# A four-layer graph network on one core: the sum of the attention exponentials moved from GpSimd to VectorE

## The reference, cut to what matters

```python
h = x @ W_sa
s_left = h @ a_sa[0, :Hd]
s_right = h @ a_sa[0, Hd:]
scores = s_left[:, None] + s_right[None, :]
e = jnp.where(adj_a != 0, jnp.exp(-jax.nn.leaky_relu(scores, 0.01)), 0.0)
attn = e / (jnp.sum(e, axis=1, keepdims=True) + 1e-05)
x_a = attn @ h
x_b = adj_b @ (x @ W_gcnb) + b_gcnb
return jax.nn.sigmoid(attn_a * x_a + attn_b * x_b)
```

## Time and profile before

| what | us |
|---|---|
| median of 3 runs | 504.92 |
| the three runs | 504.92, 501.99, 504.94 |
| the profiled execution's own time | 503.84 |
| span of its records | 502.0 |

### The profile page before, as it was taken

One profiled execution on the slowest core, in us unless ns is written; L12 is line 12 of the kernel. 1 busy time (PEld: TensorE's weight loads), 2 busy tenths in 40 slices (PEclk: granted clock), 3 DMA queues, 4 the chain that ended last, 5 costly groups with the idle time before them and its releaser, 6 DMA issues.

```text
span 502.0 us, 5846 instructions
## 1 busy us (share of the span) xinstructions
PE 481.2 (96%) x1973; PEld 319.1 (64%) x1973; DVE 349.6 (70%) x757; ACT 243.8 (49%) x448; POOL 173.1 (34%) x175
## 2 busy tenths in 40 slices
PE   5999999999999989999999999999999999999994
PEld 4889855545555678878545445555556645878782
DVE  4589879999963569849233952972752289699984
ACT  5766549992877353433334533442433466343200
POOL 1421242460534028934000631451240055355531
PEclk9999999999999999999999999999999999999998
DMA  8757120000453000000000000000000000000000
GB/s 300 235 170 215 40 83 0 0 0 1 125 208 119 25 1 1 0 1 1 0 1 0 0 1 1 2 0 0 0 1 0 0 1 2 1 12 21 22 31 29
DMA packets 8149, 20.70 MB, mean 41 GB/s; under 512 B 976, under 2 KB 4708, under 8 KB 8120
## 3 DMA queue, kind: packets, MB, share of 16 engines
q1 hardware_dynamic: 6840, 18.75, 11.3%
q0 software_dynamic: 464, 0.79, 0.7%
q10 hardware_dynamic: 816, 0.79, 0.5%
HBM read 18.94 MB, written 1.39 MB: 40 GB/s over the span
## 4 chain that ended last, share of the span: by engine, by line
PE 77%; DVE 11%; issue 4%; ACT 3%; POOL 3%; DMA 1%; POOLq 0%; DVEq 0%; ACTq 0%
PE psum L1445 17%; PE psum L1227 10%; PE psum L1489 9%; PE psum L1263 9%; PE psum L1323 5%; PE psum L1555 4%; PE psum L1210 4%; PE psum L1425 4%; DVE ST L991 2%; PE psum L1282 2%; PE psum L1398 2%; PE psum L1144 2%; PE psum L1526 2%; DVE ST L987 1%; PE psum L1309 1%
## 5 line engine op out<-in xcount | busy, mean ns | idle before, releaser
L1445 PE MATMUL psum<-QT,xT 128*128 128x512 f32 (+3 forms) x264 | 108.7, 543 | 0.3 <-DVE xT L1026 0.3
L412 POOL TENSOR_TENSOR es<-es,ST 128x512 f32<-128x512 f32 (+3 forms) x60 | 72.9, 1215 | 53.7 <-ACT ST L617 52.4
L604 ACT ACTIVATE ST<-psum 128x512 f32<-128x512 f32 (+3 forms) x66 | 36.1, 547 | 84.1 <-DVE rm L965 80.3
L1445 PEld LDWEIGHTS psum<-QT,xT 128*128 128x128 f32 (+1 forms) x264 | 47.7, 186 | 40.9 <-issue 34.0
L965 DVE TENSOR_TENSOR rm<-psum,rm 128x512 f32<-128x512 f32 (+3 forms) x60 | 37.4, 624 | 41.7 <-PE psum L1445 41.4
L362 POOL TENSOR_TENSOR rstd<-veps,nhalf 128x1 f32<-128x1 f32 (+1 forms) x44 | 28.9, 658 | 94.9 <-DVE veps L772 94.8
L1555 PE MATMUL psum<-Wh,ST 128*128 128x256 f32 (+3 forms) x242 | 55.7, 381 | 1.0 <-DVE vbuf L1039 1.0
L1489 PE MATMUL psum<-ST,Wh 128*128 128x512 f32 (+3 forms) x132 | 54.4, 543 | 1.6 <-DVE vbuf L1012 1.1
L1263 PE MATMUL psum<-eb,x_all 128*128 128x512 f32 (+3 forms) x132 | 52.8, 545 | 0.0
L617 ACT ACTIVATE ST<-ST 128x512 f32<-128x512 f32 (+3 forms) x66 | 37.9, 579 | 27.4 <-DVE ST L987 24.8
L1555 PEld LDWEIGHTS psum<-Wh,ST 128*128 128x128 f32 (+3 forms) x242 | 44.3, 186 | 9.9 <-DVE vbuf L1039 1.8
(11 more groups left out here) (161 smaller groups left out, 788.2 us busy)
## 6 DMA issues: line engine op xcount, KB each, us to landing
adj_rows<-in_adj_dram SPq DMA_DIRECT2D x10, 677.0 KB, 5.6
rows<-in_adj_dram SPq DMA_DIRECT2D x10, 677.0 KB, 3.9
out_dram<-xs SPq DMA_DIRECT2D x10, 128.0 KB, 1.7
x_all<-in_x_dram SPq DMA_DIRECT2D x2, 512.0 KB, 6.8
W<-in_L_gnn_W_stack_dram SPq DMA_DIRECT2D x2, 512.0 KB, 6.2
adj_rows<-in_adj_dram SPq DMA_DIRECT2D x1, 338.5 KB
rows<-in_adj_dram SPq DMA_DIRECT2D x1, 338.5 KB
w0n<-in_L_gnn_weight_dram ACTq DMA_DIRECT2D x1, 256.0 KB, 5.2
```

The source lines that it names most:

```text
L412: nc.gpsimd.tensor_tensor(es[0:r, g % 2, 0:w], es[0:r, g % 2, 0:w], buf(g)[0:r, j, 0:w], ALU.add)\
L1445: last = nc.tensor.matmul(psum[0:r, SB[n % 3], 0:w], xT[l][:, k, j * P:j * P + r], QT[:, k, c0:c1], start=(k == 0), stop=(k == KD - 1))
```

## The change

The eleven additions to `esumb` leave GpSimd's program and enter VectorE's as `add_exps(j)`, with the same operands. Among the first six tiles `add_exps(j - 1)` stands behind `scores(j)`. `add_exps(5)` stands behind the 22 dot products and ahead of `scores(6)`. For the later tiles `add_exps(j - 1)` stands ahead of `scores(j)`, which is behind the two `zp_evac` of the round before. `add_exps(10)` stands behind the last `zp_evac` and ahead of the three `mean_mask`. The number of buffers stays at six, and the wait of `scores(j)` for `den_added` is now one for VectorE's own earlier work. TensorE's and ScalarE's programs are the same as before.

```diff
--- before.py
+++ after.py
@@ -368,16 +368,6 @@
                 r = kk(i)
                 pool.wait_ge(NA.x_ready.sem, T)
                 nc.gpsimd.tensor_scalar(xp5[0:r, i, :], x_all[0:r, i, :], 0.5, 1.0, ALU.add, ALU.mult).then_inc(xp5_ready.sem, 1)
-            for j in range(T):
-                r = kk(j)
-                pool.wait_ge(exp_ready.sem, j + 1)
-                if j == 0:
-                    nc.gpsimd.tensor_copy(esumb[:, 0:N], ebs[0][:, 0:N]).then_inc(den_added.sem, 1)
-                else:
-                    pool.wait_ge(den_added.sem, j)
-                    nc.gpsimd.tensor_tensor(esumb[0:r, 0:N], esumb[0:r, 0:N], ebs[j % RING][0:r, 0:N], ALU.add)\
-                        .then_inc(den_added.sem, 1)
-
             def low_half(i):
                 r = kk(i)
                 pool.wait_ge(xh_ready.sem, i + 1)
@@ -836,7 +826,6 @@
                 e = ebs[j % RING][0:r, 0:N]
                 if j >= RING:
                     dve.wait_ge(h_step.sem, j - RING + 1)
-                    dve.wait_ge(den_added.sem, j - RING + 1)
                 own.link(nc.vector.tensor_scalar(e, adjT[0:r, j, 0:N], 0.0, MASKED, ALU.is_equal, ALU.mult))
                 if j == 0:
                     dve.wait_ge(nslb_ready.sem, NC)
@@ -844,6 +833,17 @@
                                                         op0=ALU.add, op1=ALU.add))
                 nc.vector.scalar_tensor_tensor(out=e, in0=e, scalar=SLOPE, in1=e, op0=ALU.mult, op1=ALU.min)\
                     .then_inc(score_ready.sem, 1)
+
+            def add_exps(j):
+
+                r = kk(j)
+                dve.wait_ge(exp_ready.sem, j + 1)
+                if j == 0:
+                    nc.vector.tensor_copy(esumb[:, 0:N], ebs[0][:, 0:N]).then_inc(den_added.sem, 1)
+                else:
+                    dve.wait_ge(den_added.sem, j)
+                    nc.vector.tensor_tensor(esumb[0:r, 0:N], esumb[0:r, 0:N], ebs[j % RING][0:r, 0:N], ALU.add)\
+                        .then_inc(den_added.sem, 1)
 
             def zp_evac(i):
                 r = kk(i)
@@ -864,6 +864,8 @@
 
             for j in range(RING):
                 scores(j)
+                if j >= 1:
+                    add_exps(j - 1)
             dve.wait_ge(bias_in.sem, 16 * 6)
             for i in range(T):
                 for n in range(2):
@@ -872,6 +874,9 @@
             own.link(nc.vector.tensor_tensor(xdot[:, :, :], xdot[:, :, :], babb[:, :].unsqueeze(1).to_broadcast([P, T, 2]), ALU.add))
             i = 0
             for j in range(RING, T):
+                add_exps(j - 1)
+                if j >= RING:
+                    dve.wait_ge(den_added.sem, j - RING + 1)
                 scores(j)
                 for _ in range(2):
                     if i < T:
@@ -880,6 +885,7 @@
             while i < T:
                 zp_evac(i)
                 i += 1
+            add_exps(T - 1)
             for j in range(3):
                 mean_mask(j)
```

## The result

The changed kernel took 509.76 us (median of 4 executions, 509.60 to 511.69), the kernel before 504.74 us beside it: ratio 1.0121 (here and below a ratio of mean times), 95% interval 1.0079 to 1.0164. That is slower, and outside the range of 503.0 to 507.9 us. Ten later executions on another chip (run e8_after_again) gave 508.43 us against 503.58 us, ratio 1.0069 (1.0029 to 1.0109); the slowest of them, 511.80 us, counts as a slow run and is not in that ratio. The profiled execution took 509.90 us, with a span of 508.1 us, 6.1 us more than before.

A forecast was written before the change was run, and what follows sets the result against it. The prediction took TensorE as the bound. Its terms, 0 (GpSimd) + 0 (scores) + 1.5 us (last add), gave 505.3 us from the profiled execution and 506.4 us from the median; it forecast the middle, 505.9 us, range 503.0 to 507.9 us.

The forecast's parts named there:

- What bounds the kernel: Whole kernel: TensorE busy 481.2 of 502.0 us and 77% of the chain; no gap from 75 to 176 us.
- GpSimd, VectorE, the stretching: 75 to 176 us: GpSimd's relief gives 0; VectorE gains 16.6 us of work, loses 21.9 us of stretching.
- The relief of VectorE: Rival: VectorE's 5.3 us less busy time shortens the whole kernel, to 498.5 us; chance 0.03.
- The scores and exponentials: Tile rounds on VectorE: new waits and adds stay covered, 8.6 us of room before the last exponential is needed; cost 0.
- The last add is the one that counts: add_exps(10), between last zp_evac and masks, delays masks, attraw, tanh, hT and h_proj(0) by 1.49 us.
- Behind 176 us: After the changed stretch: every engine starts 1.5 us later and the whole stretch moves as one.
- is less than 1.49 us and runs beside it: First denominators, waiting for all eleven additions: start 1.3 us later, not added to the delay of h_proj(0).
- The sum and the range: Whole kernel: 0 + 0 + 1.5 us, forecast 505.9 us, range 503.0 to 507.9 us.
- The rivals: Last add hidden 503.8 us (0.07), GpSimd's price 506.9 us (0.06), TensorE starved 519.9 us (0.04), VectorE's relief 498.5 us (0.03).
- The one for slower: Last tile's scores: VectorE too full, exponential comes after TensorE wants it, 519.9 us; chance 0.04.

The follow-up runs named there:

- e8_after_again: The changed kernel timed again, unchanged, in ten later executions on another chip: 508.43 us against 503.58 us for the kernel before, ratio 1.0069.
- e10: Changed kernel with last addition, masks, attraw copy and coef arithmetic earlier on VectorE, denominators among h_part(9)'s matmuls: 501.98 us, ratio 0.9969 to the kernel before.
- e11: Kernel before, additions still on GpSimd, with the same reordered end of the stage as e10: 502.02 us, ratio 0.9964.
- e3: Kernel before, with TensorE's first denominators also waiting for VectorE's second mask: 510.02 us, ratio 1.0143.
- e1: Changed kernel with the last addition, add_exps(10), set ahead of the last zp_evac: 504.18 us, ratio 1.001 to the kernel before.
- e2: Changed kernel with three useless matmuls filling TensorE's idle time before the first denominators: 506.59 us, ratio 1.0067 to the kernel before.
- e9: The kernel of e7 run once more for its profile, no further change: profiled execution 504.53 us.
- e7: Changed kernel with add_exps(10) right behind zp_evac(8), attraw copy ahead of the masks, denominators among h_part(9)'s matmuls: median 503.9 us, ratio 0.9992 to the kernel before.
- e12: Changed kernel with all 22 denominator matmuls behind the last matmul of h_part(10): 505.43 us, ratio 1.003 to the kernel before.
- e5: Kernel before, with one unneeded add on VectorE between the last zp_evac and the first mask: 505.42 us, ratio 1.0025.

## Why the prediction was wrong

**What bounds the kernel.** Right, but incomplete. TensorE sets the end; what I took from the profile is that it had 0.997 of its clock, and I added up its time as if that were fixed. The three executions of the kernel before, 501.99 to 504.94 us, were a spread that I used to widen the range and did not explain. Their clocks are not on record; in the 79 later ones the spread goes with the clock, and with a second difference of 1.8 us between executions at one clock. The traced execution is itself one with the slow form of the first layer, so that the 503.84 us to which 1.5 us were added were not those of the quickest form.

**GpSimd, VectorE, the stretching.** Right. VectorE by line in the kernel after, from 67 to 170 us:

```profile
L832 DVE SCALAR_TENSOR_TENSOR eb<-nslb,nsr,eb 128x1354 f32<-128x1354 f32 (+1 forms) x11 | 17.9, 1629 | 3.9 <-ACT nslb L494 3.6
...
L845 DVE TENSOR_TENSOR esumb<-esumb,eb 128x1354 f32<-128x1354 f32 (+1 forms) x10 | 15.7, 1565 | 4.5 <-ACT eb L484 4.5
L829 DVE TENSOR_SCALAR eb<-adjT 128x1354 f32<-128x1354 f32 (+1 forms) x11 | 9.5, 860 | 1.2 <-PE psum L1269 1.2
```

The eleven L832 take 17.9 us in place of 31.4 us for L843, each 1.63 us as when undisturbed, and the ten adds 1.565 us each, for which I had 1.57 us. VectorE's 343.6 us and GpSimd's 139.8 us are what was forecast (about 344 and 139.5 us). The relief of VectorE changed nothing at the end (e10 and e11).

**The scores and exponentials.** Right. ScalarE's timeline, last exponential and the first copies of `hT`:

```profile
157.22 1.33 ACT L484 ACTIVATE eb<-eb 74x1354 f32<-74x1354 f32 x1 [4.13 <-DVE eb L834]
...
174.77 1.57 ACT L519 ACTIVATE hT<-psum 128x512 f32<-128x512 f32 x3
```

The exponential ends at 158.55 us and TensorE takes it at 167.24 us: 8.7 us of room, forecast 8.6 us.

**"The last add is the one that counts", and "Behind 176 us".** Here the prediction failed: it put the clock's part of the loss at nothing. The delays that it names came as reckoned. VectorE's timeline around the addition:

```profile
167.85 1.55 DVE L845 TENSOR_TENSOR esumb<-esumb,eb 74x1354 f32<-74x1354 f32 x1
169.32 2.40 DVE L862 TENSOR_SCALAR maskT<-adjT 128x1354 fp32r<-128x1354 f32 x3
171.64 0.17 DVE L893 COPY attraw<-attraw 128x22 f32<-128x22 f32 x1
...
180.99 0.17 DVE L908 TENSOR_SCALAR dent<-psum 128x10 f32<-128x10 f32 x1 [4.34 <-PE psum L1258]
```

The addition takes 1.55 us and puts the masks 1.47 us later, and TensorE idles for 1.29 us before the denominators, where the prediction had 1.3 us. ScalarE's `hT` begins at 174.77 us, and with the start of the stage 1.8 us earlier that is 1.5 us later than before, as reckoned. The chain of waits of the kernel after then goes another way:

```profile
167.93 1.49 DVE esumb L845
...
169.55 0.58 PE psum L1258 x4
170.12 1.67 PE psum L1269 x2
...
180.95 1.92 PE psum L1315 x4
```

It leads from the addition straight to the denominators and stays on TensorE, `h_proj(0)` at 180.95 us. The prediction said of the denominators' wait that it "is less than 1.49 us and runs beside it", and of what follows that "nothing there goes by another clock". It counted the wait as idle time only, and gave no rival in which the clock falls. What the runs showed in its place is half the clock for 13.7 us in this trace, 7.9 us of which lie behind 176 us, and that is worth some 6.5 us. TensorE so became later than `hT`, and `dent` waited 4.34 us for the denominators, though no wait of TensorE for `coef` came of that. That the idle time is what makes the loss so large is shown by e3, where a bare wait of 1.36 us cost no less, and by e1, where its absence took the loss away.

The page "TensorE: Matmul & The Clock Gate" of the Trainium skill, section "Part 1: The HAM clock gate", says that a gate sets the array's clock by how busy it has lately been, and that the moment at which the clock changes varies from run to run. The trace agrees in that the clock fell to 1.2 GHz right behind the idle time, and the executions do vary: 25 of 79 of the kernel before lie at 0.995 or more. But busy time as the profile records it does not tell the fall, since in e1 TensorE was busy for 4.00 of 4.00 us in each stretch. The page was at hand when the prediction was written and should have given a rival.

**The sum and the range.** With the clock kept, 1.5 us is about what the change costs: 503.3 and 503.6 us after against 501.7 to 502.3 us in the quickest executions before, and a stage longer by 1.47 us in e2. The rivals all lay elsewhere. The one for slower had TensorE starved of exponentials; the chance of 0.04 for slower by over 1% was far too low, the more so as the change put a wait of 1.3 us on an engine that had none there.

**What stays open.** Why an idle time of 1.07 us before the third layer's aggregate and of 1.79 us in e9 leave the clock alone, while 0.58 us before the denominators goes with larger losses of it, is not shown. That the thin work around the denominators is the reason is a guess that e7, e10, e11 and e12 fit. Those kernels moved several things at once: in e7, e10 and e11 the denominators, the wait ahead of them and the `attraw` copy, so that the earlier chain over ScalarE could have a part in the kept clock, as the later one of e5 goes with a lower clock. How much the single columns count for without the 74 rows was not tried apart either.

## What to carry to other kernels

A wait that is put on TensorE costs its own length and may also cost the clock behind it: here 1.29 us of idle time were followed by 13.7 us at half the clock. So price both, and look at the granted clock of every execution there is before calling their spread noise. A reduction that TensorE asks for at the end of a stage is best complete before TensorE asks: one addition moved ahead of a wait took away nearly all that was lost, and in the three kernels whose single-column matmuls stood among matmuls over 128 rows, 33 of 33 executions had a mean clock of 0.995 or more.

## What the runs showed of the hardware that was not expected

- The clock of TensorE fell to 0.50 while its records show it busy for 4.00 of 4.00 us (e1, 170 to 178 us), with 74-row and single-column matmuls there. That TensorE is recorded as busy does not tell that its clock stays.
- The same kernel had a mean clock of 0.987 to 0.997 from one execution to the next, and 4.9 us of difference with it (501.7 to 506.6 us).
- Eight matmuls of the first layer took 1.89 us in two of thirteen traces and 1.05 us in the others, at a granted clock recorded as 1.00 in all.
- An add on VectorE with both inputs in SBUF took 1.565 us for 1354 numbers where GpSimd needed 3.06 us, and by the prediction's estimate GpSimd's had cost VectorE 21.9 us of stretching in all.
